# Projection stages: turned jobs of the first batch ahead of all value jobs, first stack loaded behind their last store

## The reference, cut to what matters

```
# layer 0 self-attention (stage p0a) and layer 2 self-attention (stage p2a), 16 heads of 16
q, k, v = split(xn @ w_attn.T)
# layer 1 cross-attention (stage p1x): Wk makes the keys and, with another bias row, the values
q = xn @ Wq + bq;   k = ctx @ Wk + bk;   v = ctx @ Wk + bk
...
out = softmax(q @ k.T * scale) @ v
```

## Time and profile before

| | |
|---|---|
| median of 3 runs | 2302.59 us (2300.83 to 2303.88) |
| the profiled execution's own time | 2292.74 us |
| its span | 2290.9 us |
| stage p0a, first product to first product of a0a | 15.76 to 45.38 us |
| stage p1x, first product to first score of a1x | 652.73 to 703.54 us |
| stage p2a, first product to first row product of a2a | 1226.96 to 1256.21 us |

### The profile page before, as it was taken

The page is one execution under the profiler, slowest core; times in us unless marked ns, Lnnn a source line. Parts: engine busy times, 40 slices in busy tenths (PEclk is TensorE's granted clock), DMA queues, the critical chain, the costliest instruction groups (busy, mean ns, idle before and its releaser), DMA issues. The chain is left out here.

```text
span 2290.9 us, 32146 instructions
## 1 busy us (share of the span) xinstructions
PE 1857.9 (81%) x11356; PEld 937.0 (41%) x11379; DVE 1476.2 (64%) x2551; ACT 1072.9 (47%) x1818; POOL 830.4 (36%) x751
## 2 busy tenths in 40 slices
PE   5888979999785677677896787999789776999954
PEld 3444423333453444445583552333257433222223
DVE  4643266663766999985435548999454464777676
ACT  2453124444333444542344343888833433366646
POOL 1000035554245999993204012666640412000012
PEclk9999989999986989987898888999889887699977
DMA  6602551210039014003425813332044401443000
GB/s 193 162 26 87 192 174 47 65 46 1 19 103 201 15 30 78 2 1 113 156 73 186 185 54 89 80 70 49 19 176 156 142 10 34 98 95 68 10 1 19
DMA packets 172353, 190.50 MB, mean 83 GB/s; under 512 B 14820, under 2 KB 138799, under 8 KB 171287
## 3 DMA queue, kind: packets, MB, share of 16 engines
q1 hardware_dynamic: 169124, 180.07, 28.5%
q0 software_dynamic: 3072, 8.39, 1.2%
HBM read 124.04 MB, written 68.30 MB: 84 GB/s over the span
## 5 line engine op out<-in xcount | busy, mean ns | idle before, releaser
L3381 POOL TENSOR_TENSOR a2x_masked<-a2x_masked,tall_rows 128x512 f32<-128x512 f32 x128 | 163.3, 1276 | 111.4 <-ACT a2x_masked L3343 111.4
L1398 ACT ACTIVATE experts<-a1x_scores 128x1024 f32<-128x1024 f32 x128 | 124.1, 1021 | 164.5 <-PE a1x_scores L1329 164.5
L3392 DVE TENSOR_REDUCE a3x_row_most<-a3x_ring 128x1 f32<-128x512 f32 x256 | 159.3, 682 | 43.5 <-PE a3x_ring L3233 43.5
L3392 DVE TENSOR_REDUCE a2x_row_most<-a2x_ring 128x1 f32<-128x512 f32 x256 | 162.4, 679 | 7.0 <-DMA pad_scr<-wide_rows 5.3
L1435 POOL TENSOR_TENSOR a1x_tree<-experts 128x1024 f32<-128x1024 f32 x64 | 150.4, 2350 | 32.2 <-ACT experts L1398 32.2
L671 POOL TENSOR_TENSOR a0x_pair_sums<-a0x_probs_T 128x1024 f32<-128x1024 f32 x48 | 114.7, 2390 | 130.1 <-ACT a0x_probs_T L800 102.7
L854 DVE TENSOR_REDUCE ctx_then_heads<-a0x_rows 128x2 f32<-128x1024 f32 x88 | 107.7, 1224 | 82.6 <-PE a0x_rows L689 82.4
L1367 DVE TENSOR_TENSOR experts<-experts,a1x_inverse_total 128x2048 f32<-128x2048 f32 x64 | 145.7, 2276 | 4.2 <-ACT a1x_inverse_total L1411 4.2
L3336 ACT ACTIVATE a3x_probs_T<-a3x_scores_T 128x1024 f32<-128x1024 f32 x128 | 123.2, 1018 | 48.4 <-PE a3x_scores_T L3260 48.4
L1318 PE MATMUL a1x_scores<-a1x_qs,a1x_ks 96*128 96x128 bf16 x1024 | 92.4, 243 | 58.7 <-ACT experts L1398 45.1
L3336 ACT ACTIVATE wide_rows<-a2x_masked 128x1024 f32<-128x1024 f32 x128 | 135.8, 1061 | 1.4 <-POOL a2x_masked L3381 1.4
(11 more groups left out here) (676 smaller groups left out, 4268.3 us busy)
## 6 DMA issues: line engine op xcount, KB each, us to landing
v_scr<-p0x_vout SPq DMA_DIRECT2D x24, 256.0 KB, 2.0
k_scr<-p0x_x SPq DMA_DIRECT2D x24, 256.0 KB, 2.3
ctx_then_heads<-k_scr SPq DMA_DIRECT2D x8, 768.0 KB
a0x_vs<-v_scr SPq DMA_DIRECT2D x8, 768.0 KB, 5.1
experts<-in_L_ffn_w SPq DMA_DIRECT2D x8, 768.0 KB, 6.6
v_scr<-experts SPq DMA_DIRECT2D x16, 256.0 KB, 2.2
a1x_vs<-v_scr SPq DMA_DIRECT2D x16, 256.0 KB, 5.2
v_scr<-m1f_vout SPq DMA_DIRECT2D x16, 256.0 KB, 2.8
```

Of the source, the lines that this page charges most:

```text
L1398: nc.scalar.activation(ex[:, n % E, 8 * half:8 * half + 8, :], sp_[:, g % 3, :, :, :].rearrange("p i j q -> p (i j) q"), ACT.Exp).then_inc ...
L3381: nc.gpsimd.tensor_tensor(sm[:, i % 2, 1, :], sm[:, i % 2, 1, :], full[1][:, i // 2 % KT, :], ALU.add).then_inc(pool_masked, 1)
L3392: nc.vector.tensor_reduce(rm[:, u % 2, h * QT + qt:h * QT + qt + 1, part], ring[:, row_place(r) % 3, 0:n], AX.X, ALU.max).then_inc(row_mos ...
```

## The change

`half` is `n_turned // 2`. The turned jobs of batch 0 (4, in p1x 6) now have no value job beside them; all value jobs stand beside the turned jobs of batch 1. Two follow each of four turned jobs in p0a and p2a, and 3, 3, 2, 3, 3 and 2 follow the six in p1x. `first_job` becomes `half` (4, 6 and 4). SP stores the values of job i at the end of its turn, behind the part store of job i-1 and behind the loads of the first stack. In p1x the six loads go out at jobs 6, 7 and 8, two each. The padding stores of p2a move from job 4 to job 2. The stages without value jobs keep their order.

```
-    base, v_base, first_job = list(core.stored_at), list(core.v_stored_at), (n_turned // 2 + 1 if spread or not value_jobs else n_turned * 2 // 3)
-
-    beside = [[v for v in range(n_value) if v * n_turned // n_value == i] for i in range(n_turned)]
+    half = n_turned // 2
+    base, v_base, first_job = list(core.stored_at), list(core.v_stored_at), half if value_jobs else half + 1
+    beside = [[v for v in range(n_value) if half + v * (n_turned - half) // n_value == i] for i in range(n_turned)]
...
                 for i in range(n_turned):
-                    store_values(i)
                     if i >= 1:
                         store_parts(i - 1)
-                    if i == 4 and padding is not None:
+                    if i == 2 and padding is not None:
...
                         for r in range(R):
-                            sp.wait_ge(stored[r], base[r] + 16 * len(range(r, n_turned // 2, R)))
+                            sp.wait_ge(stored[r], base[r] + 16 * len(range(r, half, R)))
...
                     if i >= first_job and spread:
-                        steps, step = n_turned - first_job, i - first_job
+                        steps, step = half // 2, i - first_job
                         prefetch(sp, first[len(first) * step // steps:len(first) * (step + 1) // steps], core.first_in)
+                    store_values(i)
                 store_parts(n_turned - 1)
```

## The result

| | before | changed |
|---|---|---|
| median of 4 runs each | 2303.24 us (2300.83 to 2306.02) | 2319.38 us (2311.42 to 2321.41) |
| the profiled execution's own time | 2292.74 us | 2311.42 us |
| its span | 2290.9 us | 2309.6 us |
| p1x, first product to first score | 50.8 us | 63.5 us |
| p0a, first product to stack 1 asked for | 33.5 us | 33.5 us |

The account below looks back on a forecast made before the run. In p1x the prediction took PE as pacemaker, then a tail with full DMA engines and the first stack 5.3 us late. Terms 14.0 + 2.3 + 2.9 = 19.2 on the 2302.6 us median gave 2321.8 us, range 2311 to 2331.

Parts of the forecast that it names:

- p1x, +14.0: p1x: loads start 7 us earlier, but value stores behind them make a chain; +14.0 us, bounds +3 and +21.
- The landing behind loads: p1x: value stores with loads ahead of them take 5.2 us to land, in three groups.
- The 3.0 for the other two: p1x: value stores with only one part store ahead take 3.0 us to land.
- p0a, +2.3: p0a: the value ring delays the stage's end, so stack 1 is asked for later; +2.3 us, bounds 0 and +3.8.
- p2a, +2.9: p2a: the same as in p0a, stack 1 asked for at 36.5 against 33.6; +2.9 us, bounds 0 and +5.
- The padding stores at job 2: p2a: four small issues while SP waits for parts cost nothing; 2.4 us at most without that cover.
- The first stack wins: Rival, p1x: the ring doesn't bite and the first score comes 5.3 us earlier; 2297.3 us, chance 0.03.
- round 1: p1x: the first value stores leave at 26.3 us and land at 31.5; the next stores go at 36.0.
- Quick landings: Rival: landings near 2.0 us; p1x costs 3 to 4, p0a and p2a about 1 each; 2308 us, chance 0.1.
- The clock falls in the gaps: Rival, p1x: PE's pauses lower the clock and slow turned jobs, up to 5 us more; 2326.8 us, chance 0.2.
- No change: Rival: the shifts are taken up by unseen waits in a0a, a1x and a2a; 2302.6 us, chance 0.03.
- The rule on early DMAs: p1x: issue a DMA early, wait late; by that rule alone the sum would be a gain of 5.3 us.

Follow-up runs that it names:

- p1x alone: The changed kernel with the old order in p0a and p2a, so only p1x is changed: 2317.39 us, ratio 1.0072.
- the kernel before again: A second measurement of the kernel before, line for line the same, meant to test new slots alone: 2301.91 us, ratio 1.0005.
- the short stages alone: The changed kernel with the old order in p1x, so only p0a and p2a are changed: 2304.93 us, ratio 1.0017.
- the loads last: The changed kernel with p1x's six first-stack loads issued behind the last part store: 2324.73 us, ratio 1.0105.
- the ring of four: The changed kernel with four value slots in p1x instead of three, and five part slots: 2319.58 us, ratio 1.0096.
- two steps and a ring of four: The kernel before with p1x's six loads at jobs 7 and 8, four value slots and five part slots: 2295.16 us, ratio 0.9995.

## Why the prediction was right

**p1x, +14.0: the mechanism, its place and its size.** The forecast assumed a start at the low clock, so it is held against "p1x alone", which had one. Forecast and measured, from the first product: first loads 25.0 and 25.5; first value stores 26.3 and 26.8; the next groups 36.0, 45.1, 52.7, 58.7 and 37.0, 46.6, 53.1, 59.0; first score 65.6 and 66.7. The landing behind loads was taken at 5.2 in three rounds; it is 5.6 to 6.0 in the first two and 4.1 in the third. The 3.0 for the other two is 2.8 to 3.0. The rounding down from the computed 14.8 to 14.0, on the ground that the landings stood at their long end, went the wrong way: like for like the term is 66.7 - 51.2 = 15.5, as the two traces of the old order that began at 0.50 as well (the kernel before again, and the short stages alone) both have 51.2. In the profiled execution of the changed kernel it is 12.7, because that one began at the full clock.

**p0a, +2.3: about right.** The trace of the changed kernel shows 0.0 to 0.6, which looks like a miss. But its first four products were quick (20 in 8.82 us) and those of the kernel before slow (3.75 us for 4, 1.9 us lost). "Short stages alone" starts slowly as well and shows 1.8 for the asking, 2.5 for the use. Two readings in this term were off and cost little: stack 1 was asked for at 33.5 before, not 33.9 (so the steps as written give +2.7), and the 3.8 us of the earlier trace rows are the first of the two value stores behind the loads; the second took 4.5.

**p2a, +2.9: too small.** Measured are 3.7 and 4.0, and 4.3 and 5.0 with the short stages alone, at the bound of 5. Over all traces, p2a with the old order asks for stack 1 at 33.4 to 34.5 and with the new at 36.8 to 37.9, so the term is about 3.5. The step that fell short is "The padding stores at job 2 are four small issues while SP waits for parts anyway: nothing". SP's cover was there, POOL's was not. Without value jobs between them the turned jobs come faster, and POOL, which also makes the padding row in this stretch, is late for them:

```profile
1259.81 0.62 ACT L374 CAST p2a_hml<-p2a_left 128x512 bf16<-128x512 f32 x1 [3.85 <-POOL p2a_left L400]
```

The wait for POOL there was 1.22 us in the kernel before. One trace allows a price: with the loads last, p0a and p2a start equally slowly (20 products in 11.04 and 11.24 us), and their first loads go out at +18.5 and +20.6, so the stage with the padding row is 2.1 us later; in the kernel before the two are at +22.0 and +22.3. That POOL's wait is the whole difference is argued, not tested.

**The sum: closer than its terms.** Like for like the three stages cost about 15.5, 2 and 3.5 us, 21 in sum, where 19.2 was forecast; between the medians it is 16.1, with an interval of 9 to 20. So the terms were a little small, and the whole came out smaller than they add up to. Why is open, and that 2321.8 is only 2.4 us from the measured 2319.38 is in part luck: four runs of each kernel can't fix the whole to better than some 5 us.

**The rivals.** "The first stack wins" fell: round 1 wants its slots at once and waits 6.23 us. "Quick landings" fell in p1x: 5.6 and more behind loads. "The clock falls in the gaps" came half true: the clock fell to 0.50 from 680 to 690, but DVE then waited at 694.11 for a store and not for PE, so at that point the slow products were hidden behind the landing. "No change" fell with the ratio.

**The rule on early DMAs.** The Trainium skill, page "DMA: Bandwidth & Descriptors", section "Queues, rings and completion order", says that each DMA engine takes the descriptors of one issuing queue in their order. The runs agree: the same value stores land in 3.0 us with the loads behind them and in 5.8 with the loads ahead. (That the two merely share the DMA engines would look alike here; no run tells them apart.) That is the other half of the rule that the prediction weighed: a load issued early is early at the cost of the stores behind it.

## What to carry to other kernels

Before a load is moved forward, list what stands behind it in the same issuing queue, and ask for each whether a buffer slot waits for it. A store's landing is free while its ring has slots to spare. It costs up to a full round trip per group when a group is as wide as the ring and loads stand ahead of its stores: 9.9 us per group here, 5.9 without the loads, and 5.9 is also what wide groups take with no wait for a store at all. Room for two groups took the loss away (six slots for threes; four gave 2 us, five were not tried). Where the ring can't grow, issue the stores first: here that single line took back the loss, as far as the whole can show it.

## What the runs showed of the hardware

- **The clock at a stage's start varies between executions.** Four products at the start of p1x take 1.95 us at a granted clock of 1.00 or 3.75 us at 0.50, and it moves the first score by 3.2 us. The changed kernel, the ring of four and the loads last have the same instructions up to this point, and began p1x at 1.00, 0.57 and 0.56; two executions of the kernel before began it at 0.58 and 0.50. A comparison of two profiled executions has to be read with it. The Trainium skill, page "TensorE: Matmul & The Clock Gate", section "Part 1: The HAM clock gate (the "warmup" mystery)", says that the number of slow first matmuls differs between runs of one kernel; the traces agree.
- **The granted clock is not always what the products show.** In p0a of the kernel before, four products took 3.75 us while the column for 15 to 21 us reads 1.00.
- **A landing behind loads has no fixed size.** Value stores took 5.6 to 6.0 us behind two loads in the changed kernel. With two steps and a ring of four they stand behind six loads, and took 7.7 to 9.1. SP's timeline, and the landing of the four value stores of 690 to 694 us:

```profile
683.20 1.97 SPq L140 DMA_DIRECT2D a1x_qs<-q_scr  x3
...
686.33 4.29 SPq L140 DMA_DIRECT2D a1x_ks<-k_scr  x3
```

```profile
DMA to landing us min/median/max: 7.7/8.2/9.1
```

Issuing itself gets longer too: 4.29 us for three loads, where the three before them took 1.97.
